# A recommender tower on one core: GpSimd's gathers held at no point, and fewer products of ones ahead of the look-ups

## The reference

```python
e = jnp.stack([tbl_f[ids[:, f]] for f in range(26)], axis=1)      # 26 looked-up rows per sample
combined = jnp.concatenate((dense[:, None, :], e), axis=1)        # 512 x 27 x 128
interactions = jnp.einsum('bfd,bgd->bfg', combined, combined)
z = jnp.concatenate((dense, interactions[:, iu, ju]), axis=1)     # 351 pairs, triu k=1
h = jnp.concatenate([z, dense], axis=1)                           # 607 columns
h = jnp.maximum(h @ W_top1 + b_top1, 0.0)                         # 512
h = jnp.maximum(h @ W_top2 + b_top2, 0.0)                         # 256
y = h @ W_top3                                                    # 1
```

## Time and profile before

| | us |
|---|---|
| median of 3 runs | 125.9 |
| lowest and highest | 124.06, 126.88 |
| the profiled execution | 124.81 |
| its span, first to last instruction | 123.0 |
| TensorE busy, of the span | 104.2 (85%) |
| GpSimd busy, of the span | 65.7 (53%) |
| VectorE busy, of the span | 65.4 (53%) |
| ScalarE busy, of the span | 48.1 (39%) |

### The profile page before, as it was taken

The page is one execution under the profiler, slowest core; times in us unless marked ns, Lnnn a source line. Parts: engine busy times, 40 slices in busy tenths (PEclk is TensorE's granted clock), DMA queues, the critical chain, the costliest instruction groups (busy, mean ns, idle before and its releaser), DMA issues.

```text
span 123.0 us, 3436 instructions
## 1 busy us (share of the span) xinstructions
PE 104.2 (85%) x1516; PEld 87.9 (71%) x1516; DVE 65.4 (53%) x110; ACT 48.1 (39%) x81; POOL 65.7 (53%) x66
## 2 busy tenths in 40 slices
PE   6999999999999999962178996289995299998993
PEld 6787888888888888831067895177992278996991
DVE  2599999999899996820001742105540106451411
ACT  4542979197794931300000462002541102730321
POOL 3887888579878887877500887503778305000000
PEclk9999999999999999999555999756999558999999
DMA  3799999999211112121200111200112100000000
GB/s 57 236 400 365 402 398 408 410 392 368 80 43 45 45 43 48 44 63 43 64 5 5 43 43 43 64 0 0 45 43 64 43 0 20 23 0 0 0 0 1
DMA packets 3949, 13.51 MB, mean 110 GB/s; under 512 B 1315, under 2 KB 1317, under 8 KB 3302
## 3 DMA queue, kind: packets, MB, share of 16 engines
q1 hardware_dynamic: 2018, 9.48, 20.5%
q0 software_dynamic: 1920, 3.94, 11.2%
q10 hardware_dynamic: 4, 0.00, 0.0%
HBM read 13.42 MB, written 0.00 MB: 109 GB/s over the span
## 4 chain that ended last, share of the span: by engine, by line
PE 83%; issue 13%; DVE 2%; ACT 1%
PE bank L365 17%; PE prod L408 13%; PE bank L414 13%; PE prod L365 12%; PE bank L374 7%; PE bank L504 6%; PE prod L433 4%; PE bank L321 4%; PE bank L325 3%; PE bank L445 2%; DVE inter_s L585 1%; PE bank L438 1%; PE prod L421 1%; PE bank L421 0%; DVE xT L575 0%
## 5 line engine op out<-in xcount | busy, mean ns | idle before, releaser
L313 POOL DMA_INDIRECT emb<-in_tbl,ids_sb x60 | 65.0, 1083 | 38.3 <-PE prod L408 19.3
L522 DVE TENSOR_SCALAR mask<-ids_h,ids_sb 128x1024 fp32r<-128x1024 int16 (+1 forms) x48 | 31.5, 699 | 2.2 <-issue 0.8
L408 PE MATMUL prod<-xT 128*27 128x27 f32 x1024 | 16.8, 215 | 14.7 <-issue 14.2
L408 PEld LDWEIGHTS prod<-xT 128*27 128x27 f32 x1024 | 13.6, 128 | 18.8 <-issue 17.4
L585 DVE STREAM_TRANSPOSE inter_s<-prod 128x288 f32<-128x288 f32 (+1 forms) x8 | 4.6, 611 | 26.3 <-PE prod L408 26.3
L365 PE MATMUL bank<-mask,high 128*128 128x512 f32 x46 | 15.2, 393 | 0.0
L365 PE MATMUL bank<-mask,low 128*128 128x512 f32 x46 | 15.0, 390 | 0.0
L414 PE MATMUL bank<-pairs,w_sb 117*128 117x128 f32 x96 | 12.7, 282 | 0.1
L414 PEld LDWEIGHTS bank<-pairs,w_sb 117*128 117x128 f32 x96 | 11.6, 191 | 0.7 <-ACT pairs L696 0.5
L531 DVE TENSOR_TENSOR low<-table,high 128x1024 fp32r<-128x1024 f32 (+1 forms) x9 | 11.7, 1301 | 0.0
L374 PE MATMUL bank<-ident,emb 128*128 128x128 f32 x60 | 10.5, 310 | 0.9 <-issue 0.9
(11 more groups left out here) (55 smaller groups left out, 118.1 us busy)
## 6 DMA issues: line engine op xcount, KB each, us to landing
table<-in_resident SPq DMA_DIRECT2D x3, 1024.0 KB
w_sb<-in_weights SPq DMA_DIRECT2D x1, 1792.0 KB
table<-in_resident SPq DMA_DIRECT2D x1, 1280.0 KB
table<-in_resident SPq DMA_DIRECT2D x4, 256.0 KB
emb<-in_tbl,ids_sb POOLq DMA_INDIRECT x60
ids_h<-in_other_ids SPq DMA_DIRECT2D x1, 896.0 KB
table<-in_resident SPq DMA_DIRECT2D x1, 640.0 KB
ids_h<-in_pair_ids SPq DMA_DIRECT2D x1, 256.0 KB
```

Source lines behind the costliest of these rows:

```text
L313: nc.gpsimd.indirect_dma_start(out=rows(t, c), out_offset=None, in_=gathered[c], in_offset=bass.IndirectOffsetOnAxis(ap=ids_sb[:, i:i + 1] ...
L408: mm = nc.tensor.matmul(prod[SLOT_PITCH * q:SLOT_PITCH * q + SLOTS, i, 0:SLOTS], x, x, start=True, stop=True)
L522: nc.vector.tensor_scalar(made(step)[:, 0:n, :], ids_h[:, 2 * b:2 * b + n, :], col_sb[:, row:row + 1], None, ALU.is_equal).then_inc(s_mask, 1)
```

## The change

`hold` and its call go: GpSimd issues its 60 gathers one behind the other, with the wait on `s_tr` alone. Of the products of ones, the four ahead of the spreading become three, now with 128 moving columns instead of 64, and the seven behind it become two such products and six with 32 stationary and 32 moving columns.

```diff
-WARM_UP, WARM_KEEP = 4, 7
-WARM_COLUMNS = 64
+WARM_UP, WARM_KEEP, WARM_NARROW = 3, 2, 6
+NARROW = 32
...
-            def hold(t, i):
-
-
-                if (t, i) == (1, 0):
-                    pool.wait_ge(s_used, first_step[2])
-                if (t, i) == (1, 8):
-                    pool.wait_ge(s_used, first_step[3] + 2)
-                if (t, i) == (2, 0):
-                    pool.wait_ge(s_used, first_step[4] + 3)
-                if (t, i) == (2, 6):
-                    pool.wait_ge(s_used, first_step[5] + 3)
-                if (t, i) == (2, 10):
-                    pool.wait_ge(s_prod, 1)
-                if (t, i) == (3, 0):
-                    pool.wait_ge(s_l1, 2)
-                if (t, i) == (3, 4):
-                    pool.wait_ge(s_prod, 2)
-                if (t, i) == (3, 9):
-                    pool.wait_ge(s_l1, 4)
-                if (t, i) == (3, 13):
-                    pool.wait_ge(s_prod, 3)
-
             for t in range(TILES):
                 for g, (first, n) in enumerate(GROUPS):
                     if t >= 2:
 
                         pool.wait_ge(s_tr, NG * (t - 2) + g + 1)
                     for c in range(first, first + n):
-                        hold(t, c)
                         i = t * GATHERED + c
...
-            def keep_busy(n):
+            def keep_busy(n, rows=P):
                 for _ in range(n):
-                    nc.tensor.matmul(half_bank[1][:, 0:WARM_COLUMNS], warm, warm[:, 0:WARM_COLUMNS], start=True, stop=True)
+                    nc.tensor.matmul(half_bank[1][0:rows, 0:rows], warm[:, 0:rows], warm[:, 0:rows], start=True, stop=True)
...
             spread()
             keep_busy(WARM_KEEP)
+            keep_busy(WARM_NARROW, NARROW)
             look_up_first()
```

## The result

| | before | after |
|---|---|---|
| median of 4 runs, us | 125.9 | 138.6 |
| lowest and highest | 124.06, 126.88 | 133.91, 147.11 |
| the profiled execution, its span | 124.81, 123.0 | 133.91, 132.1 |

The change makes the kernel slower: ratio 1.07, 95% interval 1.049 to 1.091. Two of the four runs after (143.0 and 147.1) and one of the four before (126.88) fell in a disturbed, slower state and are not in the ratio; the other two after took 133.91 and 134.15. The forecast was 134, with a span of 131.5.

What follows compares the result with a forecast made beforehand. Bound by TensorE's own work and its holes beside gathers, 17.8 us in passes 1 to 3. 4.8 + 5.0 + 2 + 2.9 - 6.2 = +8.5 on 124.81 gives 133.3, forecast as 134 on the median's scale; own range 129 to 137.

Steps and rivals of the forecast that it cites:

- Holds in the look-ups: Look-ups: only gather 15's hold shows; without it later gathers come 0.70 us earlier, with 0 effect on the end.
- Gathers 40 to 44: Pass 1's first half: these gathers no longer wait for pass 1's products, so the half ends at 68.1, +4.8 us.
- the wider products (look-ups, layers) run beside gathers unharmed: Look-ups and layers: only small products, 13 ns a record, slow to 2 to 3 records a us beside gathers.
- Gathers 45 to 48 in the second half: Pass 1's second half: these gathers now run beside it and stall it until 75.75, +5.0 us, the largest doubtful term.
- Rival 1: Passes: only the half that opens a pass stalls, so pass 1's second half loses nothing; 127.5 us, chance 0.17.
- The clock behind it: Layers of pass 1: the stall delays the clock's return, so part of them runs slow; +2 us, bounds 0 and 4.
- Gathers 49 to 59: Pass 2's first half: it stalls until these gathers land at 95.0 and ends at 96.3, +2.9 us.
- Rival 2: Head of a pass: a stall of fixed length, about 5 us, if gathers are then being issued; 119.0 us, chance 0.12.
- Pass 3: Pass 3: no gather is left, its first half falls from 6.6 to about 1.5 us and the clock stays up; -6.2.
- Ones: Start: fewer products of ones let look-ups begin at 5.7 us, first run ending -0.7 (bounds -1.5, +1.3); 0 at the end.
- Rival 3: Passes: the holes have nothing to do with gathers, so only the changed products of ones act; 125.0 us, chance 0.13.
- the law behind the forecast: Products of the passes: beside gathers in flight they give only 2 to 3 records a us until the rows land.

Runs made afterwards that it cites:

- experiment 3: Changed kernel with the one hold of gather 15 put back, which did nothing: 133.1 us, ratio 1.068 to the kernel before.
- experiment 1: Kernel before with all holds removed and its old products of ones kept: 133.0 us against 124.6, ratio 1.072.
- experiment 2: Changed kernel with all holds put back, so only the products of ones differ from the kernel before: 125.3 us against 124.6, ratio 1.005.
- experiment 11: The changed kernel run again, unaltered, beside the kernel before: 132.8 us against 124.4, ratio 1.069.
- experiment 4: Kernel before with the 15 gathers of tile 0 alone, the other tiles turning tile 0's rows again: 103.6 us against 124.6.
- experiment 10: Kernel before with the last hold one gather earlier, on gather 57 and not 58: 107.0 us against 107.0, ratio 1.001.
- experiment 7: Kernel before with eight more fulfilled waits per look-up step behind the first pair, all gathers, 125 us condition: 125.3 us against 124.4, ratio 1.011.
- experiment 5: Kernel before with eight more fulfilled waits per look-up step behind the first pair, all gathers, 107 us condition: 108.5 us against 107.0, ratio 1.015.
- experiment 6: Kernel before with eight more fulfilled waits per look-up step behind the first pair and tile 0's gathers alone, 107 us condition: 106.2 us.
- experiment 8: Kernel before with plain copies of 128 rows in place of the gathers of tiles 1 to 3: 104.4 us against 107.0, ratio 0.976.
- experiment 9: Kernel before with plain copies for the gathers of tiles 1 to 3, run in the fourth session: 103.4 us against 107.0, ratio 0.973.
- experiment 12: Changed kernel with three of eleven holds put back, those of gathers 40, 49 and 58: 106.1 us against 107.0, ratio 0.999.

## Why the prediction was right, and where its reasons were not

The time (134 forecast, 133.91 and 134.15 measured), the sign, and the span to 0.6 us are right. That the sum is so near is in part luck: the terms were +4.8, +5.0, +2, +2.9 and -6.2, and the same stretches measure +6.9, +4.4, +1.2, +3.2 and -6.1, with -0.6 for the rest of pass 2. Step by step:

1. *Holds in the look-ups.* Right on GpSimd (no idle over 0.31 us up to gather 44) and on the end. With the changed ones the hold of gather 15 would not have bound at all (experiment 3).
2. *Gathers 40 to 44.* Gather 44 was issued at 63.94, forecast 64.9; its rows had landed by 66.1, forecast 67.2. Pass 1's first half ended at 70.2, forecast 68.1 (+6.9 for +4.8). The size is right to 2 us and the place is wrong: the time was lost in the look-ups. (The prediction gives this half as 10.56 us before the change; that is the stretch from 53.00 to 63.56. The half itself took 9.6, from which the 8.0 lost follow.) The step that failed is the reading "the wider products (look-ups, layers) run beside gathers unharmed". Four profiles (after, and experiments 1, 2 and 11) have stops of over 1 us in the look-ups. That the kernel before showed none in its one profile was its luck, not a rule. The end came later than forecast because VectorE's copy began only at 68.07, 4.6 us after the last look-up's last product began and 2 us after gather 44's rows had landed. It waits for the count of that look-up and for nothing else, and all 128 records of the half came behind it, where the forecast had 70 of them done by the landing.
3. *Gathers 45 to 48 in the second half.* This was the largest doubtful term: +5.0. The half lasted 6.1 us for 1.65 of work, so 4.5 were lost; from the end of the first half to the end of the second it took 8.4 us instead of 3.9. Rival 1, only the half that opens a pass stalls, is refuted by that hole:

```profile
73.10:77.60 4.50, 1.08 (x23) 0.86 (x23) 0.00 (x0) 0.00 (x0) 2.84 (x3) 0.85 0.24 58
```

   23 records in 4.5 us, with rows at 58 GB/s.
4. *The clock behind it.* +2 forecast. From the end of the second half to pass 2's start are 9.0 us (78.57 to 87.60), before 7.8 (67.22 to 75.00): +1.2.
5. *Gathers 49 to 59.* The last was issued at 93.56, forecast 92.7. Pass 2's first half took 9.8 us, before 6.6: +3.2, forecast +2.9. It ended at 97.4, forecast 96.3. Rival 2, a stall of fixed length (4.9 us and 1.65 of work from 87.6), would have ended it at about 94.
6. *Pass 3.* Its first half fell from 6.7 to 1.5 us, and from there to pass 4's start are 9.8 us instead of 10.8: -6.1, forecast -6.2. Its first row is in the chain above, at 107.99.
7. *Ones.* The look-ups began at 5.84, forecast 5.7; the first pair ended 1.25 us earlier (14.85 for 16.10), and nothing of it reached the end. Experiment 2 measured the same: 1.005.

Rival 3, that the holes have nothing to do with gathers, is refuted by experiment 4: 21 us go with the gathers of three tiles, which is the forecast's 17.8 and the clock's share. But the law behind the forecast, rows in flight make TensorE slow, holds at this strength only in one of two conditions of the machine, and experiment 10 shows next to nothing of it in the other. It was luck that the runs shown before came from the same condition as those after.

Shown, in the 125 us condition: the loss is the holds' alone, and without the gathers of tiles 1 to 3 the holes don't come (experiment 4). That it is the rows in flight and not GpSimd's issuing of them rests on the ends: but for such pauses as in experiment 1, the holes in the products end when the last rows land, 1.9 to 2.9 us after the last gather began. Shown too: in the look-ups the count of finished steps reaches the other engines microseconds after the records, and no fixed place in the code starts a hole. Seen three times and not tested by an experiment: a pause or lull of 1.6 us or more in the rows' traffic goes with the end of a hole. Refuted: a form of product that alone stalls, a stall of fixed length, and starving by the count of instructions. Not shown: that TensorE is starved of instructions at all. In the look-ups its stops are waits for masks, which speaks neither for it nor against it. In the products it stops with no wait in the program, and its records come in bursts about 0.7 us apart, which fits a starved engine but no run tests it. What sets the condition stays open.

## What to carry to other kernels

When an engine has holes with no cause in the profile, lay the other queues' rows beside them and read when the holes end; that end gave this forecast its terms, although the cause was never found. Then read in the program what the engine waits for, and set the time at which each wait was released beside the record that should have released it: "issue" stood here on steps that began 0.05 us after their mask. Do not infer from one profile which work is immune: ask for a run in which the suspected neighbour is absent, and for a second profile of the same kernel. And let each comparison bring its own runs of the kernel before, since the same binary took 124.6 and 107.0 us on one chip within half an hour.

## What the runs showed of the hardware that was not expected

- The kernel before has two levels, medians of 124.4 to 125.9 us and of 107.0 us, each steady through a whole session (7, 23, 7 and 13 runs), and one chip showed both. At 107 us gathers in flight cost little: 108.5 us with all of them against 106.2 without three quarters, both with the extra waits.
- In the 125 us condition, with gathers in flight, TensorE gives in its holes one step of two products about every 2.1 us in the look-ups, or 1 to 6 small records at a time in the products, mostly 0.7 or 1.4 us apart.
- In that condition TensorE's count for the last look-up reached VectorE 4.60, 6.92 and 4.72 us after the last product began (after, experiments 3 and 7); it took 0.42 or 0.43 us in the kernel before and in experiments 2, 4 to 6, 8 to 10 and 12.
- 352 more fulfilled waits on TensorE, in 44 steps, cost 0.9 us in the 125 us condition and 1.5 in the 107 us one.
